# Three PSUM banks for the output product, a later second-row turn, and two operand splits moved one stage on

## The chip, the cores and the metric

The kernel runs on one core of one Trainium2 chip. The metric is the device time of one execution in microseconds, and kernels are compared by their medians. TensorE (PE in the profile) multiplies and transposes, VectorE (DVE), ScalarE (ACT) and GpSimd (POOL) do elementwise work, SyncE (SP) issues most of the transfers.

## The reference, cut to what matters

The reference is a two-layer transformer block on four sequences of 256 tokens with 256 features (1024 tokens, eight tiles of 128). Cut to the part that matters here:

```python
xn = layernorm(x)
x  = x + L0_attn(xn) + L0_ffn(xn)      # latent attention, 32 experts with top-4
xn = layernorm(x)                      # "second rows"
x  = x + L1_attn(xn) + L1_ffn(xn)
# L0_attn ends in   attn.reshape(B, S, H * D_V) @ o_w.T          (the output product)
# L0_ffn  ends in   out[tok] += expert_row * weight              (four rows a token)
# L1_attn begins    q, k, v = xn @ Wq.T, xn @ Wk.T, xn @ Wv.T ;  q, k = rope(q), rope(k)
#                   km = k.reshape(B, nblk, CHUNK, H, d).mean(2) ;  gate = q . km
# L1_ffn  begins    logits = xn @ Wg.T ;  a1 = xn @ A1.T ;  a3 = xn @ A3.T   (low-rank input)
```

## The kernel before, in words

Everything is one hand-ordered program. Each engine has its own list of instructions, and the lists meet only in semaphores. An engine runs its list in order, so an instruction that waits holds up all that stands behind it on that engine. The change touches the seam between the two layers, which has three stages.

**Output stage** (tiles i = 0 to 7). TensorE sums eight matmuls (in `output_part`) into `bank[i % 2]`, so it may begin tile i only when VectorE has added tile i - 2 (`op_add`). Tile 0 and the first three of tile 1 are mostly done earlier (`EARLY`). VectorE, per tile, adds two weighted expert rows (the pair at L1669), adds the row that GpSimd has summed from the other two (L1673, waits for `res_summed`), adds the output product (L1676), takes mean and variance (L1678, L1680) and forms scale and shift of the tile before (L1651, L1653). ScalarE weights the rows that GpSimd sums (`results_weighted`, L1116), takes the square root (L1134) and writes the normalised rows `xn1` (`normal1`, L1121). GpSimd sums two rows a tile (L884).

**Turns.** Two tiles of `xn1` at a time are transposed by TensorE (`turn1(g)`, g = 8 to 11, banks 2 and 3). ScalarE copies each result twice (`x1_copies`, L1127 and L1128: a rounded high part and the whole), and VectorE subtracts to get the low part (`x1_low`, L1659). Before, g = 8, 9, 10 are turned behind tiles 3, 5, 7 of the output product and g = 11 in the next stage.

**Splits of weights.** The float32 products of the next stage are made from rounded high and low parts. `w_qkvg` and `a13` (the low-rank input weights) are split by ScalarE (high, L1143) and GpSimd (low, L889), in the output stage: ScalarE at tiles 3 and 4, GpSimd behind its row sums of tiles 4, 5 (`w_qkvg_lo`) and 6, 7 (`a13_lo`).

**Next stage (queries, keys, values).** For each tile TensorE runs twelve matmuls (L2161) into banks 4 and 5 or 6 and 7. Tile i needs the low parts of its rows (`xt_lo`) and the rotation (L1700 to L1703 on VectorE) of tile i - 2. ScalarE copies the values out (L1153). GpSimd adds the two halves of the rotation (L897), TensorE transposes the sums (L2168), ScalarE copies them (L1157), VectorE reduces the keys to block means (L1714, L1721). In between TensorE runs eight "low" fills (L2189), the products of the rows with `a13`, four ahead of the block products (L2178) and four behind them. The first of them waits for both halves of `a13_lo`:

```python
                if what == "low":
                    if n == 0:
                        pe.wait_ge(w_low, W_SPLITS + 2 * KD)
```

Behind the block products come their masking (L1753, L1756), the comparisons that rank blocks (L691, L700, L702) and the attention of the second layer, whose first step on VectorE (L1774) needs the comparisons done and `own_bias` of ScalarE (L1178).

Of the kernel before, what the change touches and what calls it, by code (L numbers as in the profile page):

```python
# [14 lines left out]
ALU = mybir.AluOpType  # L15
ACT = mybir.ActivationFunctionType
AX = mybir.AxisListType

P = 128
B, S, D = 4, 256, 256  # L20
TOK = B * S
NT = TOK // P
QT = S // P
KD = D // P
# [97 lines left out]
W_SPLITS = SU_STEPS  # L122
# [3 lines left out]
HALF = NT // 2  # L126
HOT = 8
EARLY = {0: ((0, 0, 5),), 2: ((0, 5, 7), (1, 0, 1)), 3: ((1, 1, 3),)}
EARLY_DONE = {0: 7, 1: 3}
KEPT = TOPK0 // 2  # L130
FIRST_TURNS = {2 * NF - 3: (0, 1), 2 * NF - 1: (2, 3)}
DOWN_BANK, DOWN_AFTER = (0, 1, 2, 3, 0, 3, 1, 2), (0, 0, 0, 0, 1, 4, 2, 3)
# [158 lines left out]
def at_least(eng, sem, n):  # L291

    if not isinstance(n, int) or n > 0:
        eng.wait_ge(sem, n)


def program(nc, t, y):

    ctx = ExitStack()
    with ctx:  # L300
# [321 lines left out]
        def r(ap):  # L622
            return ap.bitcast(F32R)
# [177 lines left out]
        def _(pool):  # L801
# [79 lines left out]
            for i in range(NT):  # L881
                at = TILE_AT[i] * TOPK0 + KEPT
                pool.wait_ge(res_weighted, i + 1)
                pool.tensor_tensor(picked[:, at, :], picked[:, at, :], picked[:, at + 1, :], ALU.add).then_inc(res_summed, 1)  # L884
                if i >= HALF:
                    n, k = (i - HALF) // KD, (i - HALF) % KD
                    raw, hi, lo = ((w_qkvg, w_qkvg_hi, w_qkvg_lo), (a13, a13_hi, a13_lo))[n]
                    pool.wait_ge(w_high, W_SPLITS + n + 1)
                    pool.tensor_tensor(r(lo[:, k]), raw[:, k], hi[:, k], ALU.subtract).then_inc(w_low, 1)  # L889
            pool.wait_ge(op_mm, NT)  # L890
            pool.memset(kmean, 0.0).then_inc(kmean_set, 1)
            pool.wait_ge(op_add, NT)
# [2 lines left out]
            for i in range(NT):  # L895
                pool.wait_ge(rope_mul, 3 * i + 3)
                pool.tensor_tensor(qk_tok[:, i, :], rope_tmp[:, i % 2, 0, :], rope_tmp[:, i % 2, 1, :], ALU.add)\  # L897
                    .then_inc(rope_add, 1)

            ranks_b = rank.rearrange("p (b q) (h n) -> p q b h n", q=QT, n=NB)  # L900
            for q in range(QT):
                pool.tensor_copy(ranks_b[:, q], along(table("later", QT, NB)[:, q], (1, B), (2, H1))).then_inc(kmean_set, 1)
# [57 lines left out]
        def _(act):  # L960
# [163 lines left out]
            def x1_copies(g):  # L1124
                act.wait_ge(turned, g + 1)
                src, cols = bank[turn_bank(g)][:, :].rearrange("p (k n) -> p k n", k=KD), slice((g % 4) * 2 * P, (g % 4 + 1) * 2 * P)
                act.activation(r(x1T_hi[:, :, cols]), src, ACT.Copy)  # L1127
                act.activation(x1T[:, :, cols], src, ACT.Copy).then_inc(turned_out, 1)  # L1128
# [3 lines left out]
            for i in range(NT):  # L1132
                act.wait_ge(ln_mv, NT + i + 1)
                act.activation(sd[:, i:i + 1], mv[:, i, 1:2], ACT.Sqrt, bias=table("eps_norm")).then_inc(ln_sd, 1)  # L1134
                if i + 2 < NT:
                    results_weighted(i + 2)
                if i:
                    normal1(i - 1)
                if i in (3, 4):
                    if i == 3:  # L1140
                        act.wait_ge(ab_in, 32)
                    raw, hi = ((w_qkvg, w_qkvg_hi), (a13, a13_hi))[i - 3]
                    act.activation(r(hi), raw, ACT.Copy).then_inc(w_high, 1)  # L1143
                if i in (3, 5, 7):
                    x1_copies(8 + (i - 3) // 2)
            normal1(NT - 1)
            act.wait_ge(op_add, NT)
            for i in range(NT):
                if i == 4:
                    x1_copies(11)  # L1150
                act.wait_ge(qkv_mm, i + 1)
                src = bank[5 + 2 * (i % 2)]
                act.activation(v_one[i][:, :, 0:D1], src[:, 0:D].rearrange("p (h d) -> p h d", d=D1), ACT.Copy)  # L1153
                act.activation(logit1[:, i, :], src[:, D:D + E1], ACT.Copy).then_inc(v_out, 1)
# [143 lines left out]
        def _(dve):  # L1298
# [357 lines left out]
            def x1_low(g):  # L1656
                cols = slice((g % 4) * 2 * P, (g % 4 + 1) * 2 * P)
                dve.wait_ge(turned_out, g + 1)
                dve.tensor_tensor(r(x1T_lo[:, :, cols]), bank[turn_bank(g)][:, :].rearrange("p (k n) -> p k n", k=KD),  # L1659
                                  x1T_hi[:, :, cols], ALU.subtract).then_inc(xt_lo, 1)  # L1660

            adds = KEPT + 1
            for i in range(NT):
                at = TILE_AT[i] * TOPK0
                dve.wait_ge(gathered[LANDED[i]], 16 * LANDED.count(LANDED[i]))
                for k in range(KEPT):
                    if k:
                        dve.wait_ge(combined, adds * i + k)
                    dve.scalar_tensor_tensor(acc[:, i, :], picked[:, at + k, :], weight4[:, i * TOPK0 + k:i * TOPK0 + k + 1],  # L1669
                                             acc[:, i, :], ALU.mult, ALU.add).then_inc(combined, 1)  # L1670
                dve.wait_ge(combined, adds * i + KEPT)
                dve.wait_ge(res_summed, i + 1)
                dve.tensor_tensor(acc[:, i, :], picked[:, at + KEPT, :], acc[:, i, :], ALU.add).then_inc(combined, 1)  # L1673
                dve.wait_ge(op_mm, i + 1)
                dve.wait_ge(combined, adds * (i + 1))
                dve.tensor_tensor(acc[:, i, :], bank[i % 2][:, 0:D], acc[:, i, :], ALU.add).then_inc(op_add, 1)  # L1676
                dve.wait_ge(op_add, i + 1)
                dve.bn_stats(stats[:, i, :], acc[:, i, :]).then_inc(ln_stats, 1)  # L1678
                dve.wait_ge(ln_stats, NT + i + 1)
                dve.bn_aggr(mv[:, i, :], stats[:, i, :]).then_inc(ln_mv, 1)  # L1680
                if i:
                    scale_and_shift(i - 1)
                if i in (4, 6):
                    x1_low(8 + (i - 4) // 2)
            scale_and_shift(NT - 1)
            x1_low(10)


            for i in range(NT):
                if i == 5:  # L1690
                    x1_low(11)
                dve.wait_ge(qkv_mm, i + 1)
                at_least(dve, rope_add, i - 1)
                src = bank[4 + 2 * (i % 2)][:, :].rearrange("p (h d) -> p h d", d=D1)
                cos_t = table("cos1", QT, D1)[:, i % QT, :]
                sin_t = table("sin1", QT, D1)[:, i % QT, :]
                by_cos = rope_tmp[:, i % 2, 0, :].rearrange("p (h d) -> p h d", d=D1)
                by_sin = rope_tmp[:, i % 2, 1, :].rearrange("p (h d) -> p h d", d=D1)
                half = D1 // 2
                dve.tensor_tensor(by_cos, src, along(cos_t, (1, 2 * H1)), ALU.mult).then_inc(rope_mul, 1)  # L1700
                dve.tensor_tensor(by_sin[:, :, 0:half], src[:, :, half:D1], along(sin_t[:, 0:half], (1, 2 * H1)), ALU.mult)\
                    .then_inc(rope_mul, 1)
                dve.tensor_tensor(by_sin[:, :, half:D1], src[:, :, 0:half], along(sin_t[:, half:D1], (1, 2 * H1)), ALU.mult)\  # L1703
                    .then_inc(rope_mul, 1)
# [167 lines left out]
        def _(pe):  # L1872
# [240 lines left out]

            def output_part(i, first, last):
                for p in range(first, last):
                    mm = pe.matmul(bank[i % 2][:, 0:D], ctxT[:, p, i * P:(i + 1) * P], w_vo[:, p, :],
                                   start=(p == 0), stop=(p == PAIRS - 1))
                return mm

# [20 lines left out]

            for i in range(NT):
                pe.wait_ge(at_ctx, G - UNITS + 2 * (i // QT) + 2)
                at_least(pe, op_add, i - 1)
                output_part(i, EARLY_DONE.get(i, 0), PAIRS).then_inc(op_mm, 1)
                if i in (3, 5, 7):
                    g = 8 + (i - 3) // 2
                    turn1(g, xn1, xn_done, NT + 2 * (g % 4) + 2)


            pe.wait_ge(w_low, W_SPLITS + KD)  # L2150
            for i in range(NT):
                if i == 4:
                    turn1(11, xn1, xn_done, 2 * NT)
                pe.wait_ge(xt_lo, 5 + i // 2)
                at_least(pe, rope_mul, 3 * (i - 1))
                at_least(pe, v_out, i - 1)
                tile = slice(i * P, (i + 1) * P)
                terms = [(x, w, k) for x, w in ((x1T_hi, w_qkvg_hi), (x1T_lo, w_qkvg_hi), (x1T_hi, w_qkvg_lo)) for k in range(KD)]
                for part, (a, b) in enumerate(((0, 2 * D), (2 * D, 3 * D + E1))):
                    for n, (x, w, k) in enumerate(terms):  # L2160
                        mm = pe.matmul(bank[4 + 2 * (i % 2) + part][:, 0:b - a], r(x[:, k, tile]), r(w[:, k, a:b]),  # L2161
                                       start=(n == 0), stop=(n == len(terms) - 1))
                mm.then_inc(qkv_mm, 1)
# [241 lines left out]
```

## Time and profile before

| What | Value |
|---|---|
| median of 3 runs | 700.69 us (700.65 to 703.05) |
| profiled execution, its own time | 701.29 us |
| its span, first to last instruction | 699.1 us |
| around the span | 2.2 us |
| TensorE matmul busy | 671.0 us (96%) |
| VectorE busy | 489.0 us (70%) |
| ScalarE busy | 424.3 us (61%) |
| GpSimd busy | 297.8 us (43%) |
| granted TensorE clock, mean | 1.000 |
| output stage, about | 340 to 366 us |
| next stage up to the block products, about | 366 to 395 us |

TensorE is busy nearly everywhere, so its few idle times are what a change in order can win. The stages are short and each has its own last wait, so they have to be read in the timelines, engine by engine.

### The profile page before, as it was taken

To read this page: it belongs to the slowest core of one execution; us is meant where nothing else is said; L and a number is where in the kernel's file an instruction comes from. 1 tells how busy PE (TensorE), PEld (TensorE's weight loads), DVE (VectorE), ACT (ScalarE), POOL (GpSimd) and SP (SyncE) were. 2 spreads that over 40 slices of the span, in tenths; PEclk is the share of its full clock that TensorE was granted. 3 is DMA by queue.
4 is the path that set the end of the run, shared out by engine and by line. 5 is a ranking of instruction groups with operands and counts; after the bars stand their busy time and mean duration, and the time that the engine had idled before them with its cause. 6 is when DMAs were issued, how large, how long until landed. Compare 5 with 4: busy or idle time off the path is not lost.

```text
span 699.1 us, 13847 instructions
## 1 busy us (share of the span) xinstructions
PE 671.0 (96%) x4756; PEld 581.7 (83%) x4756; DVE 489.0 (70%) x1418; ACT 424.3 (61%) x1099; POOL 297.8 (43%) x301
## 2 busy tenths in 40 slices
PE   6999999999999999999999989999989999999997
PEld 3777888888889898887787855666889999999997
DVE  6798877877877787777786886777465555644544
ACT  3766168788797878888663788888654213222221
POOL 0584154546464555542164318998334410400000
PEclk9999999999999999999999999999999999999999
DMA  8902044453535444351910000200300000000000
GB/s 329 346 1 98 1 130 121 165 166 112 168 116 165 129 152 126 101 159 59 365 79 1 1 1 2 107 1 3 121 1 1 1 1 16 2 16 1 1 16 16
DMA packets 26725, 59.43 MB, mean 85 GB/s; under 512 B 3146, under 2 KB 12748, under 8 KB 26272
## 3 DMA queue, kind: packets, MB, share of 16 engines
q1 hardware_dynamic: 23584, 50.35, 21.5%
q0 software_dynamic: 3072, 8.20, 3.6%
q8 instruction: 39, 0.64, 0.4%
q14 instruction: 30, 0.25, 0.1%
HBM read 48.24 MB, written 10.49 MB: 84 GB/s over the span
## 4 chain that ended last, share of the span: by engine, by line
PE 76%; DVE 14%; ACT 6%; issue 3%; POOL 1%; DMA 0%; DVEq 0%; ACTq 0%
PE bank L2253 11%; PE bank L2020 7%; PE bank L1954 6%; PE bank L2302 5%; PE bank L2011 5%; PE bank L2276 5%; PE bank L2040 4%; PE bank L1961 3%; PE bank L2031 3%; PE bank L2082 3%; PE bank L2316 2%; PE bank L2222 2%; PE bank L2206 2%; PE bank L1894 2%; PE bank L2161 2%
## 5 line engine op out<-in xcount | busy, mean ns | idle before, releaser
L1062 ACT ACTIVATE sb<-bank,sb 128x256 f32<-128x256 f32 x128 | 59.6, 471 | 40.6 <-DVE sb L1558 33.4
L1558 DVE TENSOR_REDUCE sb<-bank 128x2 f32<-128x512 f32 x64 | 43.7, 683 | 47.5 <-PE bank L2020 47.1
L1264 ACT ACTIVATE h_parts<-sb 128x256 fp32r<-128x256 f32 x56 | 23.4, 418 | 71.3 <-DVE sb L1809 43.4
L2020 PE MATMUL bank<-sb 128*128 128x256 f32 x256 | 66.2, 381 | 0.0
L1800 DVE TENSOR_TENSOR sb<-sb,bank 128x256 f32<-128x256 f32 x56 | 23.5, 419 | 58.1 <-ACT sb L1227 58.1
L2253 PE MATMUL bank<-rounded,b_hi 128*128 128x256 f32 x224 | 63.1, 282 | 0.0
L2253 PE MATMUL bank<-rounded,b_lo 128*128 128x256 f32 x224 | 62.9, 281 | 0.0
L2253 PE MATMUL bank<-am_lo,b_hi 128*128 128x256 f32 x224 | 62.9, 281 | 0.0
L1227 ACT ACTIVATE sb<-bank 128x256 f32<-128x256 f32 x56 | 21.5, 383 | 62.4 <-PE bank L2253 62.4
L834 POOL DMA_INDIRECT expert_out<-sb x32 | 33.0, 1032 | 61.0 <-DVE sb L1500 44.6
L1069 ACT ACTIVATE sb<-sb 128x256 f32<-128x256 f32 x128 | 57.7, 503 | 0.1
L1198 ACT ACTIVATE sb<-sb 128x128 f32<-128x128 f32 (+1 forms) x128 | 50.6, 445 | 10.1 <-DVE sb L1774 9.4
L1954 PEld LDWEIGHTS bank<-sb 128*128 128x128 f32 (+1 forms) x384 | 46.5, 186 | 5.8 <-DVE sb L1494 3.2
L828 POOL DMA_INDIRECT sb<-rows_x,sb x32 | 32.8, 1025 | 42.4 <-PE bank L1954 16.4
L1954 PE MATMUL bank<-sb 128*128 128x128 f32 (+1 forms) x384 | 48.8, 277 | 1.7 <-DVE sb L1494 1.0
L2020 PEld LDWEIGHTS bank<-sb 128*128 128x128 f32 x256 | 45.2, 190 | 4.8
L1774 DVE CUSTOM_DVE_ANT_1 sb<-bank,sb 128x128 f32<-128x128 f32 (+1 forms) x128 | 38.0, 353 | 12.8 <-ACT sb L1178 8.5
L1569 DVE TENSOR_TENSOR pt_parts<-bank,pt_parts 128x512 fp32r<-128x512 f32 x64 | 43.7, 683 | 4.5 <-ACT pt_parts L1082 3.6
L2040 PE MATMUL bank<-pt_parts,xt_parts 128*128 128x256 f32 x256 | 46.0, 302 | 0.0
L1811 DVE TENSOR_TENSOR h_parts<-sb,h_parts 128x256 fp32r<-128x256 f32 x56 | 25.9, 462 | 27.4 <-ACT h_parts L1264 27.4
L2011 PE MATMUL bank<-rounded 128*128 128x512 f32 x160 | 42.7, 399 | 0.3 <-ACT sb L1091 0.3
L2253 PEld LDWEIGHTS bank<-rounded,b_lo 128*128 128x128 f32 x224 | 42.2, 188 | 0.0
(321 smaller groups left out, 1969.9 us busy)
## 6 DMA issues: line engine op xcount, KB each, us to landing
sb<-in_w_gate_up SPq DMA_DIRECT2D x32, 368.0 KB
sb<-in_w_down SPq DMA_DIRECT2D x32, 256.0 KB
sb<-in_w_pair SPq DMA_DIRECT2D x8, 704.0 KB
expert_out<-sb SPq DMA_DIRECT2D x1, 4096.0 KB, 23.7
sb<-expert_out SPq DMA_DIRECT2D x8, 512.0 KB, 6.3
sb<-in_w SPq DMA_DIRECT2D x1, 1792.0 KB, 13.8
sb<-in_b SPq DMA_DIRECT2D x1, 1792.0 KB, 8.1
sb<-in_sw_up SPq DMA_DIRECT2D x1, 1536.0 KB, 9.4
```

The lines of the kernel that those rows point to most:

```text
L1062: act.activation(probs[:, u % 4, q, :], bank[3 + u % 2][:, q * S:(q + 1) * S], ACT.Exp, scale=-1.0, bias=row_min[:, u % 4, q:q + 1], accum ...
L1069: ins = act.activation(probs[:, slot, q, :], probs[:, slot, q, :], ACT.Copy, scale=row_inv[:, slot, q:q + 1])
L1198: act.activation(probs1[:, n % 4, a:b], masked[:, n % 4, a:b], ACT.Exp, scale=-1.0, bias=row_min[:, n % 4, q:q + 1]).then_inc(bl_exp, 1)
L1558: dve.tensor_reduce(row_min[:, u % 4, :], bank[3 + u % 2][:, :].rearrange("p (q n) -> p q n", q=QT), AX.X, ALU.min).then_inc(at_min, 1)
L1569: dve.tensor_tensor(r(probs_lo[:, u % 2]), bank[5 + u % 2][:, :].rearrange("p (a b) -> p a b", a=QT), probs_hi[:, u % 2], ALU.subtract).th ...
L1774: dve.tensor_tensor_reduce(masked[:, n % 4, a:b].rearrange("p (n c) -> p n c", c=CHUNK), bank[SCORE_BANK[n % 4]][:, a:b].rearrange("p (n c ...
L1954: mm = pe.matmul(bank[1][0:n, to:to + P], w_gu[s][:, k, a:a + n], xeT[s][:, k, :], start=(k == 0), stop=(k == KD - 1))
L2011: mm = pe.matmul(where[:, :], r(w[i][:, cols]), r(q[:, half]), start=(n == 0), stop=(n == len(terms) - 1))
L2020: mm = pe.matmul(bank[3 + u % 2][:, q * S:(q + 1) * S], qb[i][:, h, b * S + q * P:b * S + (q + 1) * P], keys[:, h, b * S:(b + 1) * S], sta ...
L2040: mm = pe.matmul(bank[2 + 5 * h][:, 0:S], r(v_parts[:, QT * b + k, :]), r(part[:, u % 2, k, :]), start=(n == 0), stop=(n == len(terms) - 1))
L2253: mm = pe.matmul(dst, lhs, rhs, start=False, stop=(n == len(terms) - 1), skip_group_check=True)
L2276: pe.matmul(dst, r(w[:, 2 * k + j, :]), r(x[:, k, :]), start=(i + j == 0), stop=False, skip_group_check=True)
```

## The change: what it does

The output product's tiles go to banks 0, 1 and 4 in turn, and tile i waits for the add of tile i - 3 in place of i - 2. TensorE waits for six adds ahead of the next stage, which writes bank 4. The turns g = 8, 9 move from behind tiles 3 and 5 to behind tiles 4 and 6, g = 10 from behind tile 7 to ahead of tile 2 of the next stage, and g = 11 stays ahead of tile 4. The copies and low parts follow. The split of `a13` leaves the output stage: its high part goes on ScalarE behind the value copy of tile 0, its low part on GpSimd behind the last rotation add.

```diff
+OUT_BANK = (0, 1, 4)
@@ GpSimd
-                if i >= HALF:
-                    n, k = (i - HALF) // KD, (i - HALF) % KD
-                    raw, hi, lo = ((w_qkvg, w_qkvg_hi, w_qkvg_lo), (a13, a13_hi, a13_lo))[n]
-                    pool.wait_ge(w_high, W_SPLITS + n + 1)
-                    pool.tensor_tensor(r(lo[:, k]), raw[:, k], hi[:, k], ALU.subtract).then_inc(w_low, 1)
+                if HALF <= i < HALF + KD:
+                    pool.wait_ge(w_high, W_SPLITS + 1)
+                    pool.tensor_tensor(r(w_qkvg_lo[:, i - HALF]), w_qkvg[:, i - HALF], w_qkvg_hi[:, i - HALF], ALU.subtract)\
+                        .then_inc(w_low, 1)
...
+            pool.wait_ge(w_high, W_SPLITS + 2)
+            for k in range(KD):
+                pool.tensor_tensor(r(a13_lo[:, k]), a13[:, k], a13_hi[:, k], ALU.subtract).then_inc(w_low, 1)
@@ ScalarE
-                if i in (3, 4):
-                    if i == 3:
-                        act.wait_ge(ab_in, 32)
-                    raw, hi = ((w_qkvg, w_qkvg_hi), (a13, a13_hi))[i - 3]
-                    act.activation(r(hi), raw, ACT.Copy).then_inc(w_high, 1)
-                if i in (3, 5, 7):
-                    x1_copies(8 + (i - 3) // 2)
+                if i == 3:
+                    act.wait_ge(ab_in, 32)
+                    act.activation(r(w_qkvg_hi), w_qkvg, ACT.Copy).then_inc(w_high, 1)
+                if i in (5, 7):
+                    x1_copies(8 + (i - 5) // 2)
...
-                if i == 4:
-                    x1_copies(11)
+                if i == 1:
+                    act.activation(r(a13_hi), a13, ACT.Copy).then_inc(w_high, 1)
+                if i in (2, 4):
+                    x1_copies(9 + i // 2)
@@ VectorE
-                dve.tensor_tensor(acc[:, i, :], bank[i % 2][:, 0:D], acc[:, i, :], ALU.add).then_inc(op_add, 1)
+                dve.tensor_tensor(acc[:, i, :], bank[OUT_BANK[i % 3]][:, 0:D], acc[:, i, :], ALU.add).then_inc(op_add, 1)
...
-                if i in (4, 6):
-                    x1_low(8 + (i - 4) // 2)
+                if i == 6:
+                    x1_low(8)
             scale_and_shift(NT - 1)
-            x1_low(10)
+            x1_low(9)
...
-                if i == 5:
-                    x1_low(11)
+                if i in (2, 5):
+                    x1_low(10 + i // 5)
@@ TensorE
-                    mm = pe.matmul(bank[i % 2][:, 0:D], ctxT[:, p, i * P:(i + 1) * P], w_vo[:, p, :],
+                    mm = pe.matmul(bank[OUT_BANK[i % 3]][:, 0:D], ctxT[:, p, i * P:(i + 1) * P], w_vo[:, p, :],
...
-                at_least(pe, op_add, i - 1)
+                at_least(pe, op_add, i - 2)
...
-                if i in (3, 5, 7):
-                    g = 8 + (i - 3) // 2
+                if i in (4, 6):
+                    g = 8 + (i - 4) // 2
...
+            pe.wait_ge(op_add, 6)
             for i in range(NT):
-                if i == 4:
-                    turn1(11, xn1, xn_done, 2 * NT)
+                if i in (2, 4):
+                    g = 9 + i // 2
+                    turn1(g, xn1, xn_done, NT + 2 * (g % 4) + 2)
```

## Rows read from the trace of the kernel before

**Rows 1.** The page, part 4: share of the chain that ended last, by engine

```profile
PE 76%; DVE 14%; ACT 6%; issue 3%; POOL 1%; DMA 0%; DVEq 0%; ACTq 0%
```

**Rows 2.** Timeline of TensorE: start us, us, engine, line, operation, count, idle before

```profile
339.13 2.75 PE L2116 MATMUL bank<-sb 128*128 128x256 f32 x12
343.14 7.14 PE L2116 MATMUL bank<-sb 128*128 128x256 f32 x32 [1.26 <-DVE sb L1676]
350.75 0.66 PE L2136 MATMUL bank<-sb 128*128 128x128 f32 x4 [0.46 <-ACT sb L1121]
...
372.45 0.70 PE L2161 MATMUL bank<-w_qkvg_hi,rounded 128*128 128x512 f32 x2 [1.52 <-DVE sb L1703]
...
385.92 3.66 PE L2168 MATMUL bank<-sb 128*128 128x128 f32 x32
389.33 0.71 PE L2189 MATMUL bank<-rounded 128*128 128x512 f32 x2
...
395.41 3.84 PE L2178 MATMUL bank<-sb 128*128 128x128 f32 x32 [0.24 <-DVE sb L1721]
```

**Rows 3.** Timeline of VectorE, output stage

```profile
347.97 0.43 DVE L1676 TENSOR_TENSOR sb<-bank,sb 128x256 f32<-128x256 f32 x1
...
350.80 0.43 DVE L1676 TENSOR_TENSOR sb<-bank,sb 128x256 f32<-128x256 f32 x1
...
352.06 1.00 DVE L1669 SCALAR_TENSOR_TENSOR sb<-sb 128x256 f32<-128x256 f32 x2
...
354.89 0.43 DVE L1676 TENSOR_TENSOR sb<-bank,sb 128x256 f32<-128x256 f32 x1 [1.36 <-PE bank L2116]
...
357.36 2.45 DVE L1669 SCALAR_TENSOR_TENSOR sb<-sb 128x256 f32<-128x256 f32 x2
359.83 0.83 DVE L1673 TENSOR_TENSOR sb<-sb 128x256 f32<-128x256 f32 x1
360.77 0.43 DVE L1676 TENSOR_TENSOR sb<-bank,sb 128x256 f32<-128x256 f32 x1
...
367.40 0.43 DVE L1676 TENSOR_TENSOR sb<-bank,sb 128x256 f32<-128x256 f32 x1
```

**Rows 4.** Timeline of GpSimd, output stage

```profile
354.99 1.83 POOL L889 TENSOR_TENSOR w_qkvg_lo<-sb,w_qkvg_hi 128x776 fp32r<-128x776 f32 x1 [3.71 <-ACT w_qkvg_hi L1143]
356.78 0.73 POOL L884 TENSOR_TENSOR sb<-sb 128x256 f32<-128x256 f32 x1
357.47 2.05 POOL L889 TENSOR_TENSOR w_qkvg_lo<-sb,w_qkvg_hi 128x776 fp32r<-128x776 f32 x1
...
360.34 1.46 POOL L889 TENSOR_TENSOR a_lo<-sb,rounded 128x512 fp32r<-128x512 f32 x1
```

**Rows 5.** Timeline of ScalarE: the high part of w_qkvg, and own_bias before the second attention

```profile
353.43 1.48 ACT L1143 ACTIVATE w_qkvg_hi<-sb 128x1552 fp32r<-128x1552 f32 x1
...
409.20 0.47 ACT L1178 ACTIVATE sb<-sb 128x128 f32<-128x128 f32 x1
```

**Rows 6.** Timeline of VectorE, next stage and behind it

```profile
370.40 0.69 DVE L1659 TENSOR_TENSOR am_lo<-bank,rounded 128x512 fp32r<-128x512 f32 x1 [1.16 <-ACT sb L1128]
...
392.93 2.43 DVE L1721 TENSOR_SCALAR sb<-sb 128x32 f32<-128x32 f32 x16
...
400.01 1.82 DVE L1756 TENSOR_TENSOR sb<-sb 128x1024 f32<-128x1024 f32 x1
...
407.94 2.56 DVE L691 TENSOR_TENSOR sb<-sb 128x672 bf16<-128x672 f32 x4
```

**Rows 7.** Timeline of GpSimd, next stage: last rotation add, and the share copies

```profile
387.55 1.27 POOL L897 TENSOR_TENSOR sb<-sb 128x512 f32<-128x512 f32 x1 [0.84 <-DVE sb L1703]
...
398.73 2.04 POOL L905 COPY sb<-sb 128x1024 f32<-128x1024 f32 x2 [8.80 <-DVE sb L1748]
```

**Rows 8.** Waits, 335 to 412 us: engine, line, released by, us in total, times, longest

```profile
ACT sb L1153 <- PE bank L2161: 11.2, 6, 3.3
```

**Rows 9.** Windows: busy of each engine, granted clock, DMA share, GB/s

```profile
515.00:525.00 10.00, 7.90 (x67) 7.73 (x66) 6.82 (x12) 5.68 (x11) 3.85 (x4) 1.00 0.01 2
```

## The prediction

> **What bounds the kernel now.** I read the chain of the page first: TensorE holds 76% of it [rows 1], so the time is TensorE's work plus the holes that others leave in it. Then the timelines of all engines from 339 to 411 us. TensorE's holes there are 1.26 us ahead of output tile 2 (bank 0 is still to be added), 0.46 ahead of the first turn, 1.52 ahead of tile 2 of the next stage, where VectorE's rotation is late, and 0.24 ahead of the block products [rows 2]. In the output stage an undisturbed VectorE needs 2.83 us a tile (350.80 less 347.97) [rows 3], TensorE 3.57 (7.14 for two) [rows 2]: TensorE is the slower, and VectorE stands idle 1.36 ahead of its add of tile 4 [rows 3]. Three bonds lead from there to the block products: the last add (367.40) to ScalarE's copies and the low part at 370.40 [rows 3, 6]; that to the rotation and TensorE at 372.45; GpSimd's last rotation add, which ends at 388.82 [rows 7] and lets the last transposes end and the fills begin at 389.33 [rows 2].
>
> **The output stage.** The third bank takes away the 1.26 us hole: tile 2 follows tile 1 at about 341.8. TensorE then ends tile 4 near 352.4 and the last tile, with two turns between at about 0.45, near 363.9 instead of 365.7. That hole alone isn't the gain: the bond that counts goes through VectorE. Its add of tile 4 comes at 350.80 + 2.83 = 353.63 instead of 354.89, 1.26 sooner.
>
> Tile 5 is where this is lost. GpSimd's first subtraction of `w_qkvg` can't move: it waits for ScalarE's high part (353.43 + 1.48) and so runs from 354.99 [rows 4, 5]. In the trace, VectorE's instructions with two inputs in SBUF stand still while GpSimd computes: the pair at L1669 takes 2.45 us beside the subtraction of 357.47, against 1.00 undisturbed, and the row add behind it 0.83 against 0.43 [rows 3, 4]. In the new order VectorE reaches the pair of tile 5 at 354.89, and the second of the two stands until 356.82, ending near 357.1. Its row add needs GpSimd's sum of tile 5, which is queued behind the first subtraction and with its own 0.73 to 0.9 ends near 357.6, and GpSimd goes straight on with the second subtraction (2.05) [rows 4]; the row add gets in when that ends and finishes near 359.9. So the add of tile 5 comes at 360.0 against 360.77, 0.77 sooner. (The Trainium skill, SBUF — State Buffer, "Who interferes with whom", has the same as an exclusive lock that the instruction first to start holds to its end. By it the second subtraction, issued without a wait, wins over a row add that needs a semaphore, and the sum stands. Were the row add to get in ahead of the second subtraction, the add of tile 5 would come near 358.3, 1.7 us sooner still: part of rival B.)
>
> From there to the last add, before: 6.63 us, two tiles at 2.83, a low part at 0.6 and 0.38 more in a shift that a subtraction of `a13` held up. New: one low part also (g = 8 in place of 9), the subtractions of `a13` gone: 6.26. The last add is at 366.3 against 367.40, g = 1.1 us sooner. Bounds: 0.4, if VectorE loses at every meeting as before; 3.5, if it loses at none (then TensorE's last tile sets the add, at 363.9).
>
> **To the rotation.** Behind the last add nothing changes but the number of the turn: square root, two copies, low part. So the low part (9 in place of 10) comes at 369.3, and tile 2 starts at 371.35 against 372.45. Turn 10 falls into the hole ahead of it; turn 11 stays. ScalarE's high part of `a13` (1.0 by the 1.48 for 1552 columns, here 1024) [rows 5] and the copies of turn 10 lie between value copies, for which ScalarE now waits 11.2 us in six waits [rows 8]: nothing, and 1.0 if that cover were gone. GpSimd's last rotation add ends at 387.7, the transposes at 388.2.
>
> **The moved subtraction.** In the output stage `a13_lo` cost nothing of its own. Now it stands behind the last rotation add, and the fills wait for both halves. One is 1.27 to 1.46 us [rows 4, 7], two with their handover 2.6, bounds 2.5 and 3.0 (VectorE may take the port first). The fills start at 387.7 + 2.6 + 0.05 = 390.4 instead of 389.33, 1.05 later, and TensorE stands idle some 2.2 us ahead of them. Four fills take 5.85; the block products start at 396.2. The block means, which are ready at 395.36 before [rows 6], come at 394.3 and no longer end last. So 395.41 becomes 396.2: 0.8 later, made of 1.85 lost ahead of the fills and 0.24 idle given back, less 1.1 won, with the transposes' tail.
>
> **Behind the block products.** The masking at L1756 has two SBUF inputs and takes 1.82 us because GpSimd copies the shares from 398.73 to 400.77 [rows 6, 7]. I estimate it undisturbed at 1.2 (0.43 for 256 columns, 0.69 for 512 with a bank, so 0.26 to 0.27 for each 256 more). The copies hang on the routing, which comes with the block means 1.1 sooner, the masking 0.8 later: they no longer meet, and 0.6 comes back. VectorE, busy without a break up to 410.50 [rows 6], is then 0.2 late. TensorE and ScalarE are 0.8 late, and `own_bias`, done at 409.67 [rows 5], is done near 410.5: just covered. Behind that the second layer moves as one piece.
>
> **Sum.** -1.1 + 1.85 + 0.05 - 0.6 = +0.2 us. On the profiled execution: 701.29 becomes 701.5, the span 699.1 becomes 699.3. That execution's own time is 0.6 above the median of the runs and 2.2 above its span, so the median goes from 700.69 to 700.9.
>
> **Rivals.**
> A, the forecast, 0.55: own range 700.1 to 702.2 (gain ahead 0.4 with masking not relieved on one side, and 1.9 on the other).
> B, 0.28: VectorE loses little to GpSimd at tile 5. Against it stands 2.45 for the pair; for it, that the meeting falls otherwise. Won ahead: up to 3.5; the subtraction still ends last, but the block products come 1.6 sooner and the masking is relieved: -0.6 to -2.2, 698.5 to 700.1.
> C, 0.08: the moved subtraction is covered, so the whole gain passes: -1.1 to -3.5, 697.2 to 699.6. Against it: program order on GpSimd and the explicit wait.
> D, 0.04, the other side: the hole of some 2.2 us ahead of the fills, behind 3.66 us of transposes, lets the granted clock fall from 2.4 to 1.2 GHz. Then the four fills take up to twice 5.85, 6.1 late in all with the rest: 706.8. It decides if the hole and the transposes together count as rest. Against it: the stretch with 2.1 us of 10 idle kept 1.00 [rows 9], as did the transposes. (The Trainium skill, TensorE: Matmul & The Clock Gate, "PE-mode transpose", says that transposes don't count as busy for the clock; no hole behind a run of transposes stands in this trace, so it speaks for D without proof.)
> E, 0.05: ScalarE, 0.8 late with the masks, isn't covered, and the masking isn't relieved, or a rotation waits on the copies: +1.5 to +3, 702.2 to 703.7.
>
> **Numbers.** A measurement of this kernel can tell about 0.5% (3.5 us) from no change: below 697.2 and above 704.2. Of C and B only the far ends reach the lower bound, so faster 0.04; D and a tail of E, slower 0.04; the same 0.92. Range for 8 in 10: from the middle of B to the upper end of A and a part of E, 699.0 to 702.8.
>
> **What the profile after would show.** No idle ahead of output tile 2. VectorE's add of tile 4 at 353.6, of tile 5 near 360.0, of tile 7 near 366.3. A pair at L1669 or a row add at L1673 of over 1.8 us beside the first or second subtraction. Tile 2 of the next stage at 371.3. TensorE idle about 2.2 us ahead of the first fill, released by GpSimd's `a13_lo`. L1756 near 1.2 us. I am wrong if the fills start before 389.3 (B or C), if that idle is named after another engine, or if the clock there is below 1.00 (D).

## The result, and the profile after

| | before | after |
|---|---|---|
| median of 22 runs each | 700.87 us (700.07 to 703.05) | 702.7 us (699.99 to 703.16) |
| ratio of the run times, 95% interval | | 1.0018 [1.0011, 1.0025] |
| profiled execution, its own time and span | 701.29, 699.1 us | 703.16, 700.8 us |
| mean granted clock of the profiled execution | 1.000 | 0.995 |

The change is 1.3 us slower by the ratio (0.0018 of 700.87); the medians lie 1.8 us apart. The interval excludes no change, but the difference is below the 0.5% that was set as "the same". The median lies inside the forecast range of 699.0 to 702.8, close to its upper end and 1.8 us above the forecast of 700.9. Of the 22 executions of the changed kernel 17 have a mean clock of 0.995 and a median of 702.8; the three with 1.000 took 701.22 to 701.28. The kernel before isn't free of this: of 76 executions of it beside the experiments 38 have 1.000, 22 have 0.998 or 0.999, and 16 have 0.995 or less.

The two traces don't reach the output stage at the same time: VectorE's first add comes at 342.57 before and at 342.07 after (341.11 to 342.63 over all traces here). So distances are taken from that add. First the chain of the page after, its shares by engine; TensorE's share was 76% [rows 1]:

```profile
PE 73%; DVE 15%; ACT 5%; issue 4%; POOL 1%; DMA 0%; DVEq 0%; ACTq 0%
```

TensorE's timeline after, the rows that answer to [rows 2]:

```profile
338.63 13.11 PE L2119 MATMUL bank<-sb 128*128 128x256 f32 x60
...
364.52 0.70 PE L2166 MATMUL bank<-w_qkvg_hi,rounded 128*128 128x512 f32 x2 [1.55 <-DVE am_lo L1662]
...
370.90 0.70 PE L2166 MATMUL bank<-w_qkvg_hi,rounded 128*128 128x512 f32 x2 [1.45 <-DVE sb L1706]
...
384.37 3.66 PE L2173 MATMUL bank<-sb 128*128 128x128 f32 x32
389.87 0.70 PE L2194 MATMUL bank<-rounded 128*128 128x512 f32 x2 [1.84 <-POOL a_lo L902]
390.40 0.63 PE L2194 MATMUL bank<-am_lo,rounded 128*128 128x512 f32 x2
390.87 1.01 PE L2194 MATMUL bank<-rounded,a_lo 128*128 128x512 f32 x2
391.68 1.05 PE L2194 MATMUL bank<-rounded 128*128 128x512 f32 x2
...
397.08 3.73 PE L2183 MATMUL bank<-sb 128*128 128x128 f32 x32
```

Sixty matmuls run without a hole where one of 1.26 us lay. A hole of 1.55 us now stands ahead of tile 0 of the next stage, where TensorE waits for VectorE's low part of turn 8: TensorE got ahead, and it is VectorE that sets the pace. The new hole ahead of the first fill is 1.84 us long and released by GpSimd's low part of `a13`. Behind it something else is to be seen: a pair of fill matmuls takes 0.63 us, then 1.01 and 1.05. The windows after name it (columns as in [rows 9]; the clock is the third number from the end):

```profile
390.00:393.00 3.00, 3.00 (x10) 2.34 (x11) 2.96 (x13) 1.98 (x5) 0.83 (x2) 0.65 0.03 5
393.00:396.00 3.00, 3.00 (x12) 2.38 (x11) 2.90 (x32) 0.72 (x2) 0.00 (x0) 0.78 0.00 0
524.00:527.00 3.00, 3.00 (x16) 3.00 (x15) 1.56 (x2) 0.98 (x3) 2.25 (x2) 0.50 0.00 0
```

TensorE's clock fell from 2.4 to 1.2 GHz for part of the fills, and once more at 524 us (0.50), behind a hole of 2.10 us near 520 that every version has but the last below. In the trace before, both stretches ran at 1.00. A mean clock of 0.995 goes with two such falls in the traces of after and a13_only, one of 0.997 or 0.998 with a single fall; the mean doesn't say where a fall lies.

VectorE's timeline after, for [rows 3, 6]:

```profile
342.07 0.43 DVE L1679 TENSOR_TENSOR sb<-bank,sb 128x256 f32<-128x256 f32 x1
...
353.12 0.43 DVE L1679 TENSOR_TENSOR sb<-bank,sb 128x256 f32<-128x256 f32 x1
...
354.39 2.45 DVE L1672 SCALAR_TENSOR_TENSOR sb<-sb 128x256 f32<-128x256 f32 x2
357.53 1.97 DVE L1676 TENSOR_TENSOR sb<-sb 128x256 f32<-128x256 f32 x1 [0.69 <-POOL sb L885]
359.61 0.42 DVE L1679 TENSOR_TENSOR sb<-bank,sb 128x256 f32<-128x256 f32 x1
...
365.86 0.43 DVE L1679 TENSOR_TENSOR sb<-bank,sb 128x256 f32<-128x256 f32 x1
...
401.58 1.22 DVE L1759 TENSOR_TENSOR sb<-sb 128x1024 f32<-128x1024 f32 x1
```

And GpSimd's after, for [rows 4, 7]:

```profile
354.49 2.07 POOL L888 TENSOR_TENSOR w_qkvg_lo<-sb,w_qkvg_hi 128x776 fp32r<-128x776 f32 x1 [3.71 <-ACT w_qkvg_hi L1144]
356.52 0.90 POOL L885 TENSOR_TENSOR sb<-sb 128x256 f32<-128x256 f32 x1
357.39 1.83 POOL L888 TENSOR_TENSOR w_qkvg_lo<-sb,w_qkvg_hi 128x776 fp32r<-128x776 f32 x1
...
387.23 2.49 POOL L902 TENSOR_TENSOR a_lo<-sb,rounded 128x512 fp32r<-128x512 f32 x2
```

Read the two together: VectorE's row add of tile 5 first waits 0.69 us for the sum that stands behind the first subtraction, then starts at 357.53, just behind GpSimd's second subtraction of 357.39, and ends at 359.50, 0.28 us behind that one's end at 359.22. The 1.97 us hold an add that takes 0.43 undisturbed. The pair ahead of it (2.45) ends at 356.84, 0.28 us behind the first subtraction (356.56).

### The profile page after: what moved, and what is told of

Read it like the earlier page. It is cut to its first block, busy times and chain, and to the rows that moved or that the text cites. A ratio compares the mean times of both kernels' runs of the same rounds, so it can differ in the third digit from the quotient of the medians.

```text
span 700.8 us, 13846 instructions
## 1 busy us (share of the span) xinstructions
PE 672.7 (96%) x4756; PEld 584.4 (83%) x4756; DVE 488.7 (70%) x1418; ACT 424.5 (61%) x1099; POOL 297.6 (42%) x301
## 4 chain that ended last, share of the span: by engine, by line
PE 73%; DVE 15%; ACT 5%; issue 4%; POOL 1%; DMA 0%; DVEq 0%; ACTq 0%
PE bank L2258 11%; PE bank L2023 7%; PE bank L1957 6%; PE bank L2281 5%; PE bank L2014 5%; PE bank L2307 5%; PE bank L2043 3%; PE bank L1964 3%; PE bank L2034 3%; PE bank L2085 3%; PE bank L2321 2%; PE bank L2227 2%; PE bank L2166 2%; PE bank L1897 2%; PE bank L2211 2%
```

## The experiments

The kernels ran on four occasions, each time with the kernel before on the same chip; the ratios are to those runs. All distances are in us from the first add of the same trace. "Rest" is from the first step of the second attention on VectorE to the end of the span.

| trace | last add | tile 2 | first fill | block products | second attention | rest |
|---|---|---|---|---|---|---|
| before | 24.83 | 29.88 | 46.76 | 52.84 | 67.86 | 288.67 |
| after | 23.79 | 28.83 | 47.80 | 55.01 | 69.31 | 289.42 |
| a13_back | 24.59 | 29.63 | 46.49 | 52.58 | 67.58 | 288.56 |
| a13_only | 24.47 | 29.50 | 48.48 | 55.70 | 70.00 | 289.53 |
| no_hole | 23.80 | 28.84 | 45.72 | 51.81 | 66.81 | 288.58 |
| warm | 23.81 | 28.85 | 47.76 | 53.46 | 67.80 | 288.58 |
| banks_only | 25.48 | 30.52 | 47.42 | 53.51 | 68.51 | 288.66 |
| sum_first | 22.66 | 27.70 | 46.71 | 52.37 | 66.70 | 289.43 |
| both_fixes | 22.66 | 27.71 | 44.58 | 50.67 | 65.68 | 289.49 |
| warm_late | 22.68 | 27.72 | 44.61 | 50.70 | 65.71 | 288.64 |

**One part undone: the split of `a13` back in the output stage.**

```diff
-                if HALF <= i < HALF + KD:        # GpSimd: w_qkvg alone, a13 behind the last rotation add
+                if i >= HALF:                    # GpSimd: w_qkvg at tiles 4, 5 and a13 at 6, 7
...
-                if i == 3:                       # ScalarE
+                if i in (3, 4):
```

> The changed kernel with the split of a13 put back into the output stage (high part on ScalarE at tile 4, low parts on GpSimd behind the row sums of tiles 6 and 7); banks and turns stay changed. Theory 1 (the moved subtraction opens a hole ahead of the first fill, and the hole lets the TensorE clock fall): no idle of over 0.3 us ahead of the first fill, clock 1.00 there, but GpSimd stops VectorE at tiles 6 and 7 again, so tile 2 of the next stage starts 0.5 to 2 us later than the changed kernel's 370.9; time 700.4 to 701.5, 1.2 to 2.3 us under the changed kernel. Rival (the clock falls for another reason, such as the steadier output stage drawing more): clock still 0.995, time 701.5 to 703.

Measured 701.07 us, ratio 1.0003 [0.9994, 1.0012], 1.05 us under the changed kernel by the ratios, a little less than expected. No hole ahead of the fills, clock 1.00 there in the trace, and tile 2 is 0.8 us later than in the changed kernel. So the banks and the turns without the split are worth 0.26 us at the block products (52.58 against 52.84), which the runs can't tell from nothing. In six of its eleven executions the mean clock was 0.993 or 0.997, so falls aren't tied to the hole ahead of the fills alone. Its trace also has a longer hole, ahead of tile 0 of the next stage, and the clock didn't fall behind it; first TensorE's timeline, then the windows:

```profile
365.72 0.69 PE L2164 MATMUL bank<-w_qkvg_hi,rounded 128*128 128x512 f32 x2 [2.34 <-DVE am_lo L1660]
```

```profile
364.00:367.00 3.00, 1.28 (x6) 1.10 (x7) 2.77 (x9) 0.84 (x2) 1.53 (x2) 1.00 0.01 3
367.00:370.00 3.00, 3.00 (x20) 2.67 (x19) 1.56 (x7) 1.81 (x5) 0.33 (x2) 1.00 0.00 0
```

**That part alone, in the kernel before.** ScalarE's high part moves with it, behind the value copy of tile 0.

```diff
+            pool.wait_ge(w_high, W_SPLITS + 2)   # GpSimd, behind the rotation adds
+            for k in range(KD):
+                pool.tensor_tensor(r(a13_lo[:, k]), a13[:, k], a13_hi[:, k], ALU.subtract).then_inc(w_low, 1)
```

> The kernel before with the split of a13 alone moved behind the last rotation add; banks and turns as before. Theory 1: TensorE idle of 1.8 to 2.3 us ahead of the first fill, clock down for about 3.4 us behind it in most executions, block products some 2 us (clock kept) to 3.5 us (clock fallen) later than 395.4, of which the masking gives back 0.6; time 701.9 to 703.8. Rival (the hole costs only its own length, the clock falls by the new banks and turns): clock 1.000, 701.4 to 702.3.

Measured 701.93 us, ratio 1.0015 [1.0004, 1.0026]: within the noise the whole loss of the change. Its trace has the same hole and the same fall:

```profile
391.05 0.70 PE L2191 MATMUL bank<-rounded 128*128 128x512 f32 x2 [1.84 <-POOL a_lo L901]
```

```profile
393.00:396.00 3.00, 3.00 (x10) 2.33 (x9) 2.90 (x22) 0.93 (x2) 0.00 (x0) 0.59 0.00 0
```

The first is TensorE's timeline, the second a window with clock 0.59. Five of its eleven executions had a mean clock of 0.995 and took 702.98 to 704.35 us, the others (0.998 or 0.999) 701.11 to 701.93. The median alone would fit the rival too (701.4 to 702.3); what makes it fall is the clock, which it had at 1.000 and which no execution shows, and the fall in the trace without the new banks and turns.

**The hole filled with thrown-away work.** The order and the waits stay.

```diff
                     if n == 0:
+                        pe.wait_ge(w_high, W_SPLITS + 2)
+                        for m_ in range(7):
+                            pe.matmul(dst[:, :], r(a13_hi[:, 0, 0:P]), r(x1T_hi[:, 0, 0:CH]), start=True, stop=True,
+                                      skip_group_check=True)
                         pe.wait_ge(w_low, W_SPLITS + 2 * KD)
```

> The changed kernel with seven extra matmuls (128 by 512, their result thrown away) between the last transpose and the wait for a13_lo, so that the hole is filled with work and the order and the waits stay. Theory 1: the fills start at the same time as in the changed kernel (389.9), clock 1.00 from 390 to 394, block products at 395.7 in place of 397.1; time 701.0 to 702.0, 0.8 to 1.7 us under the changed kernel. Rival (filling the hole doesn't matter to the clock): clock 0.995, time as the changed kernel's, 702.7 within 0.4.

Measured 700.64 us, ratio 0.9995 [0.9986, 1.0004]: more work, and 0.0023 faster than the changed kernel by the ratios, 1.6 us (0.4 us below the expected range). TensorE's timeline:

```profile
387.04 1.88 PE L2192 MATMUL bank<-rounded 128*128 128x512 f32 x7
389.08 0.73 PE L2198 MATMUL bank<-rounded 128*128 128x512 f32 x2 [0.17 <-POOL a_lo L902]
```

The fills start as far behind the first add as in the changed kernel (47.76 and 47.80), and then take 5.70 us to the block products in place of 7.21. Only the work in the hole differs, and the clock stays at 1.00 in this trace. The fall costs 1.5 us at this place, and still 1.51 at the second attention (69.31 less 67.80). Seven of eleven executions had a mean clock of 1.000, where the changed kernel had three of 22: this count and the ratios show that filling the hole is what keeps the clock up.

**The hole covered with the fills' own work.** The four matmuls of each fill that read the high part go ahead of the wait for the low part, for all four fills.

```diff
                     if n == 0:
+                        pe.wait_ge(w_high, W_SPLITS + 2)
+                        for m_ in range(4):
+                            low_terms(m_, 0, 2 * KD)
                         pe.wait_ge(w_low, W_SPLITS + 2 * KD)
...
+                    mm = low_terms(n, 2 * KD if n < 4 else 0, 3 * KD)
```

> The changed kernel, with the matmuls of the first four fills in another order: the four of each that need only the high part of a13 go first for all four fills (banks 4 to 7), and only then comes the wait for a13_lo. Same work. Theory 1: first fill right behind the transposes, the wait is covered by 3.7 us of matmuls, no clock fall there, block products near 394.0 against 397.1, set by the block means again; masking meets GpSimd's copies in part; time 699.2 to 700.3, under both kernels. Rival (a fall of the clock by something else, such as the run of transposes): clock 0.998 or less between 390 and 394, time 700.5 to 702.

Measured 699.07 us, ratio 0.9979 [0.9970, 0.9988], 0.1 us below the expected range. TensorE's timeline:

```profile
386.83 0.72 PE L2182 MATMUL bank<-rounded 128*128 128x512 f32 x2
...
392.92 3.84 PE L2193 MATMUL bank<-sb 128*128 128x128 f32 x32 [0.25 <-DVE sb L1724]
```

No wait ahead of the first fill, and the block products wait 0.25 us for the block means again, as before the change. They come 1.03 us sooner than in the kernel before, which is what the output stage won (24.83 less 23.80).

**The third bank alone, in the kernel before.**

```diff
-                at_least(pe, op_add, i - 1)
+                at_least(pe, op_add, i - 2)      # with OUT_BANK = (0, 1, 4) and the wait for six adds; turns and splits as before
```

> The kernel before with the three banks alone (and the wait for six adds ahead of the next stage); turns and splits as before. Theory 1: the hole of 1.26 us ahead of output tile 2 goes, but turn 8 stands behind tile 3 and waits for rows that VectorE and ScalarE end when they did, so the hole comes back ahead of that turn (0.46 us becomes 1.7) and everything behind stays: block products 52.8 us behind the first add as before, time within 0.3 us of the kernel before. Rival (a hole of TensorE that is removed is time won, whatever stands next): 1.2 us sooner, 699.6.

Measured 701.63 us, ratio 1.0005 [0.9993, 1.0017]. The hole went ahead of tile 2 and came back ahead of the turn:

```profile
350.81 0.76 PE L2137 MATMUL bank<-sb 128*128 128x128 f32 x4 [1.95 <-ACT sb L1122]
351.36 8.70 PE L2117 MATMUL bank<-sb 128*128 128x256 f32 x32
```

1.95 us instead of 0.46 [rows 2]: nothing won, as expected, and the rival's 699.6 falls. The second row wasn't expected: tiles 4 and 5 take 8.70 us in place of the 7.07 of this row of the trace before, where the hole ahead of the turn was 0.46:

```profile
351.24 7.07 PE L2116 MATMUL bank<-sb 128*128 128x256 f32 x32
```

The window from 351 to 357 us has a clock of 0.72 in this execution, and 1.00 in the trace before. With it the block products come 53.51 us behind the first add, 0.7 later than the expected 52.8.

**GpSimd's subtractions one row sum later.**

```diff
-                if HALF <= i < HALF + KD:
+                if HALF < i <= HALF + KD:        # and the indices one lower
```

> The changed kernel with GpSimd's two subtractions of w_qkvg each one row sum later (behind the sums of tiles 5 and 6 in place of 4 and 5). Same work. Theory 1 (at tile 5 VectorE's row add stands behind GpSimd twice: its sum is queued behind the first subtraction, and the second subtraction then holds the port): the row add of tile 5 isn't held by the second subtraction, the adds of tiles 5 and 7 come 15.2 and 21.8 us behind the first add in place of 17.5 and 23.8, and with the hole ahead of the fills still there the time is 1.5 to 2.2 us under the changed kernel's, 700.5 to 701.2 in executions with a fallen clock, 699.0 to 699.7 with a full one. Rival (the order of two instructions on GpSimd makes no difference, since the port is held the same time in all): adds as in the changed kernel, 701.2 to 702.7.

Measured 701.02 us, ratio 0.9996 [0.9987, 1.0005], against 1.0018 of the changed kernel: 1.5 us less. VectorE's timeline:

```profile
354.18 2.46 DVE L1672 SCALAR_TENSOR_TENSOR sb<-sb 128x256 f32<-128x256 f32 x2
356.67 0.83 DVE L1676 TENSOR_TENSOR sb<-sb 128x256 f32<-128x256 f32 x1
357.61 0.43 DVE L1679 TENSOR_TENSOR sb<-bank,sb 128x256 f32<-128x256 f32 x1
```

The row add of tile 5 takes 0.83 us in place of 0.69 of waiting and 1.97, so the add comes at 15.74 (expected 15.2) in place of 17.54. The last add comes at 22.66, expected 21.8: the sums of tiles 6 and 7 now each hold a row add (0.83 for 0.43), and the second subtraction holds a shift (0.41 for 0.16), which I had not counted. The mechanism held, half of its size didn't: 1.1 us in place of 2.0. The rival (order makes no difference) falls. This trace has the hole ahead of the fills too, behind the same 3.66 us of transposes, and the clock stayed at 1.00; TensorE's timeline and the window:

```profile
388.58 0.70 PE L2194 MATMUL bank<-rounded 128*128 128x512 f32 x2 [1.86 <-POOL a_lo L902]
```

```profile
391.00:394.00 3.00, 3.00 (x14) 2.42 (x13) 2.90 (x26) 1.20 (x2) 0.00 (x0) 1.00 0.00 0
```

The fills take 5.66 us here (46.71 to 52.37) and 7.21 in the changed kernel, with the same hole ahead: what costs the 1.5 us is the fall and not the hole.

**Both repairs:** the edits of no_hole and sum_first together.

> The changed kernel with both repairs: GpSimd's subtractions one row sum later, and the four fills' matmuls on the high part of a13 ahead of the wait for its low part. Theory 1: the two gains add: 699.07 of the run without a hole, less 1.5 to 2.0: 697.0 to 697.6, clock 1.00 between 385 and 395. Rival (with the rows sooner another engine ends last, such as ScalarE's copies of the turns): 698.0 to 699.1.

Measured 698.77 us, ratio 0.9959 [0.9946, 0.9972], faster than both kernels, though still within 0.5% of the kernel before. The expected 697.0 to 697.6 was missed, for two reasons: the later subtractions give 1.1 and not 2.0, and the rest is 289.49 in place of 288.6. The time lies in the rival's range (698.0 to 699.1), but not for its reason: against no_hole the last add and the block products both come 1.14 us sooner (22.66 for 23.80, 50.67 for 51.81), so no other engine took the gain away. TensorE's timeline and the windows behind it:

```profile
518.99 0.48 PE L2291 MATMUL bank<-x_hi,w_hi_rest 128*128 128x256 f32 x2 [2.10 <-DVE sb L1803]
```

```profile
518.00:521.00 3.00, 2.01 (x12) 2.04 (x13) 2.45 (x6) 1.03 (x3) 0.40 (x1) 0.78 0.00 0
521.00:524.00 3.00, 3.00 (x19) 3.00 (x19) 0.81 (x1) 0.38 (x1) 2.08 (x2) 0.66 0.00 0
```

The hole of 2.10 us, which the kernel before has as well, let the clock fall in this execution. All five have a mean clock of 0.997 or 0.998, so each had a fall somewhere.

**That hole filled too.** Fifteen matmuls into an unused bank ahead of the wait of the sixth step of the last stage.

```diff
+                if n == 5:
+                    pe.wait_ge(bl_o, QUADS)
+                    for m_ in range(15):
+                        pe.matmul(bank[2][:, 0:CW], r(w13_hi[4][:, 0, :]), r(x1_hi[0][:, 0, :]), start=True, stop=True,
+                                  skip_group_check=True)
```

> The kernel with both repairs, and fifteen extra matmuls (128 by 256, result thrown away) in the hole of 2.1 us that TensorE has near 520 us in every version, ahead of the sixth step of the last stage, while it waits for VectorE. Theory 1 (any hole of about 2 us can let the clock fall, and each fall costs 0.8 to 1.5 us): clock 1.000 in nearly all executions and behind 520 us none of the 0.85 us that the second part of the both_fixes execution lost; median 697.7 to 698.3, against 698.77. Rival (that fall hangs on something else, such as the mix of the last stage): clock 0.998 and 698.5 to 699.0 as in both_fixes.

Measured 698.72 us, ratio 0.9958 [0.9944, 0.9972], above the expected 697.7 to 698.3 and in the rival's range, but with the clock of theory 1. All five executions had 1.000:

```profile
517.36 1.93 PE L2286 MATMUL bank<-x_hi,w_hi_rest 128*128 128x256 f32 x15
519.54 0.51 PE L2296 MATMUL bank<-x_hi,w_hi_rest 128*128 128x256 f32 x2 [0.25 <-DVE sb L1803]
```

```profile
521.00:524.00 3.00, 2.54 (x21) 2.34 (x21) 2.33 (x4) 0.85 (x3) 2.49 (x2) 1.00 0.00 0
```

The rest is 288.64, 0.85 shorter, but the median didn't follow: this trace reached the first add at 342.15, that of both_fixes at 341.53. So the two kernels were run side by side once more.

> The kernel with both repairs once more, beside the one with matmuls in the later hole, on one chip, because 698.77 and 698.72 came from two calls while the two traces differ by 0.85 us behind the second attention's start. Theory 1: about 0.5 us above the other here, 698.3 to 699.0. Rival (the fall of the clock behind 520 us is worth nothing in the median): the two within 0.2 us.

> Both repairs and the fifteen matmuls in the hole at 520 us, beside the kernel without them. Theory 1: clock 1.000 in all executions, 697.7 to 698.5 and about 0.5 us under fixes_again. Rival: within 0.2 us of it.

Measured 698.9 us (698.5 to 699.5, 7 runs) and 698.33 us (698.09 to 698.89, 5 runs), ratios 0.9970 [0.9959, 0.9981] and 0.9964 [0.9951, 0.9978]; the rests 289.52 and 288.66 again. The 0.85 us is plain in four traces; in the run times the two intervals overlap, so there it is likely and not shown. What is plain is the clock: 11 of the 12 executions without the fifteen matmuls have a mean below 1.000, and all ten with them have 1.000.

## Why the prediction was right, and where it was short

**The output stage: right.** From the first add on, the add of tile 4 was forecast at 11.06 behind it and came at 11.05, that of tile 5 at 17.4 and came at 17.54, the last at 23.7 and came at 23.79. The trace after agrees with the lock that the Trainium skill describes (SBUF — State Buffer, "Who interferes with whom"): 1.97 us for an add of 0.43, ending 0.28 us behind GpSimd's instruction. Rival B falls by it. sum_first shows that the order on GpSimd makes 1.8 us of loss at tile 5, of which 1.1 is left at the last add.

**The way to the rotation: right.** Tile 2 was forecast 1.1 us sooner and came 1.05 sooner, as much as the last add (1.04); the moved high part on ScalarE and turn 10 cost nothing there.

**The moved subtraction: right in place and size.** The fills were forecast 1.05 us later and came 1.04 later; the idle of 1.84 us was forecast as about 2.2, and rival C falls by it. a13_only and no_hole show it from both sides. The sum's 1.85 is the loss of some 2.1 ahead of the fills less the 0.24 of idle given back; the prediction's sentence that takes the 0.24 off once more doesn't give its own 0.8.

**The masking: right.** 1.22 us for a forecast of 1.2, in place of 1.82. In the trace of warm, where the clock didn't fall, the second attention starts at 67.80, against 67.86 before: -0.06 for a forecast of +0.2. From the block products to that step it is 14.3 us in the traces of after and warm and 15.0 before, so nothing was added there and rival E falls too.

**The step that failed: "Four fills take 5.85".** They took 7.21 us (389.87 to 397.08), because the clock fell behind the hole. This was rival D, to which I gave a chance of 0.04, and its sign, a clock below 1.00 there, stood in the trace. That the median of 702.7 is inside the range all the same is luck: the upper end of 702.8 came from the end of A and a part of E, neither of which happened, and D was priced at 706.8, outside it. Seventeen of 22 executions show a mean clock of 0.995, as that trace does. I had counted the stretch with 2.1 us of idle at 1.00 [rows 9] as evidence against it, from a single execution; the same hole lets the clock fall at 524 us in the trace after, and the kernel before shows a mean below 1.000 in half of its 76 executions. The price was mis-sized the other way: 6.1 us for all fills at half speed, where the fall covers part of them and costs 1.5 us, and 0.85 at the later place (289.49 less 288.64, between traces of different kernels). 0.2 + 1.5 + 0.85 would give 703.4 for an execution with both falls; the median is 702.7, the three executions without any have 701.2, so the two falls together are worth 1.6 us in the run times and not 2.4. The Trainium skill (TensorE: Matmul & The Clock Gate, "PE-mode transpose") says that transposes don't count as busy for the clock in the same way. The fall behind 3.66 us of transposes and a hole fits that, but it isn't shown: in sum_first the clock stayed at 1.00 behind the same transposes and a hole of 1.86 us, and at 524 us (ordinary matmuls on both sides of the hole) and in banks_only (ordinary matmuls ahead of it) the clock fell with no run of transposes ahead.

**Open.** Why the same program has the fall in one execution and not in another, no run here tells. The length of the hole doesn't decide it: 2.34 us (a13_back) and 1.86 us (sum_first) kept 1.00, 1.84 us did not. The hole of 2.10 us near 520 brought a fall in the traces of after, a13_only, sum_first, both_fixes and fixes_again, and none in those of before, a13_back, no_hole, warm and banks_only. Nor is it known what a single fall costs in the run times of the kernel before: on each of the four occasions its executions with a mean clock of 0.998 were no slower than those with 1.000 (medians 0.04 to 0.5 us lower), while those with 0.995 were 0.9 to 1.6 us slower.

## What to carry to other kernels

Price a hole on TensorE with the clock as well as with its length: here 1.84 us of waiting cost 1.5 us more behind it where the clock fell, and thrown-away matmuls in the hole won that back. Look at the mean clock of many executions before a single trace is taken as proof that a hole is harmless. When an operand's low part is moved later, split the consumer too, so that the products that need only the high part go ahead of the wait. A subtraction on GpSimd is not free because GpSimd has time: look which two-input instruction of VectorE meets it, and whether the sum that VectorE waits for is queued behind it.

## What the runs showed of the hardware that was not expected

TensorE's clock is granted anew within a kernel that is busy for 96% of its span. It fell from 2.4 to 1.2 GHz behind holes of 1.84 us (389.87, after 3.66 us of transposes), 1.95 us (350.81 in banks_only) and 2.10 us (523 in the kernel after, 519 in both_fixes), and kept 1.00 behind one of 2.34 us (365.72 in a13_back), one of 2.10 us (522.18 before), one of 1.86 us (388.58 in sum_first) and one of 1.45 us (370.90 after). Matmul pairs of 512 columns went from 0.63 to 1.05 us in it. The same kernel ran with a mean clock of 0.995 in 17 and 1.000 in three of 22 executions, the kernel before with 1.000 in 38 of 76.
